# An attention and feed-forward block on one core: scores in the column tiles of the values, denominators beside the output transposes

## The reference

```
score = softmax(q k^T / sqrt(8))                # per batch and head, 1024 x 1024
out   = score v                                 # per head: 1024 x 64, seen as R = 8 rows of 8
comp  = softmax over R of ([qv, out] Ws^T + bs) # qv: 32 more query channels per head
out   = sum over R of comp * out                # 8 channels a head, 128 in all
```

## Time and profile before

| | |
|---|---|
| median of three runs | 1427.76 us |
| profiled execution, its own time | 1429.73 us |
| its span | 1428.0 us |
| PE, DVE, ACT, POOL busy | 1368.9, 1026.9, 756.1, 841.1 us |
| values, L989 | 2048 records, 558.6 us busy |
| row scores L964, column scores L981 | 1024 each, 323.6 and 313.4 us busy |
| denominators, L999 | 1024 records, 137.3 us busy |
| output transposes, L1009 | 256, 42.0 us busy |
| row maxima, L1194 | 1024, 666.5 us busy |
| exponentials, L1141 | 1024, 555.2 us busy |
| pair sums, L1294 | 256, 603.8 us busy |

### The profile page before, as it was taken

One profiled execution on the slowest core, in us unless ns is written; L12 is line 12 of the kernel. 1 busy time (PEld: TensorE's weight loads), 2 busy tenths in 40 slices (PEclk: granted clock), 3 DMA queues, 4 the chain that ended last, 5 costly groups with the idle time before them and its releaser, 6 DMA issues. The chain is left out here.

```text
span 1428.0 us, 23930 instructions
## 1 busy us (share of the span) xinstructions
PE 1368.9 (96%) x6333; PEld 436.7 (31%) x6333; DVE 1026.9 (72%) x2050; ACT 756.1 (53%) x1463; POOL 841.1 (59%) x433
## 2 busy tenths in 40 slices
PE   4699999999999999999999999999999999997898
PEld 3123222222222222222222222222222222223675
DVE  5745677877778686878777777768686868677852
ACT  4045555565555555555556555555555555563443
POOL 4235767576666766666757576665656565664321
PEclk9569999999999999999999999999999999999999
DMA  5200101010101001010101010100000000000000
GB/s 129 91 17 31 34 28 42 31 42 31 42 22 36 31 31 42 31 42 19 39 31 42 31 42 31 32 29 32 31 32 31 31 31 31 17 1 1 15 17 28
DMA packets 41937, 48.35 MB, mean 34 GB/s; under 512 B 4608, under 2 KB 23520, under 8 KB 41904
## 3 DMA queue, kind: packets, MB, share of 16 engines
q1 hardware_dynamic: 40770, 47.04, 10.0%
q0 software_dynamic: 352, 0.58, 0.3%
q10 hardware_dynamic: 782, 0.33, 0.1%
HBM read 22.51 MB, written 8.39 MB: 22 GB/s over the span
## 5 line engine op out<-in xcount | busy, mean ns | idle before, releaser
L1194 DVE TENSOR_REDUCE rowmax<-row_bank 128x1 f32<-128x512 f32 x1024 | 666.5, 684 | 319.9 <-PE row_bank L964 314.2
L1294 POOL TENSOR_TENSOR pair<-prob 128x1024 f32<-128x1024 f32 x256 | 603.8, 2359 | 452.0 <-ACT prob L1141 452.0
L1141 ACT ACTIVATE prob<-col_bank 128x512 f32<-128x512 f32 x1024 | 555.2, 594 | 463.9 <-PE col_bank L981 463.5
L989 PE MATMUL out_bank<-prob,v_op 128*64 128x512 f32 x2048 | 558.6, 624 | 0.0
L964 PE MATMUL row_bank<-k_op,q_op 72*128 72x512 bf16 x1024 | 323.6, 390 | 20.7 <-DMA v_op<-v_all 12.1
L981 PE MATMUL col_bank<-q_op,k_op 74*128 74x512 bf16 x1024 | 313.4, 387 | 0.1
L981 PEld LDWEIGHTS col_bank<-q_op,k_op 74*128 74x128 bf16 x1024 | 68.8, 98 | 332.2 <-ACT prob L1141 227.9
L989 PEld LDWEIGHTS out_bank<-prob,v_op 128*64 128x64 f32 x2048 | 101.9, 135 | 213.8 <-issue 200.5
L964 PEld LDWEIGHTS row_bank<-k_op,q_op 72*128 72x128 bf16 x1024 | 101.0, 99 | 167.6 <-DVE rowmax L1194 42.6
L999 PE MATMUL den_bank<-pair,onehot 128*32 128x512 f32 x1024 | 137.3, 608 | 0.0
L393 POOL TENSOR_TENSOR product<-mix_in,rows 128x2048 f32<-128x2048 f32 x16 | 72.5, 4529 | 2.1 <-POOLq L876 2.1
(11 more groups left out here) (183 smaller groups left out, 823.2 us busy)
## 6 DMA issues: line engine op xcount, KB each, us to landing
v_op<-v_all SPq DMA_DIRECT2D x64, 256.0 KB
k_op<-k_parts SPq DMA_DIRECT2D x64, 144.0 KB
q_op<-q_parts SPq DMA_DIRECT2D x192, 48.0 KB
q_parts<-along_parts SPq DMA_DIRECT2D x11, 192.0 KB, 2.2
k_parts<-along_parts SPq DMA_DIRECT2D x33, 64.0 KB, 2.1
out<-y_out SPq DMA_DIRECT2D x8, 256.0 KB, 2.3
q_op<-max_rows SPq DMA_DIRECT2D x64, 4.0 KB
q_parts<-first_parts SPq DMA_DIRECT2D x5, 192.0 KB, 2.1
```

The source lines that it names most:

```text
L989: last = nc.tensor.matmul(out_bank[slot % 2][ih * VW:(ih + 1) * VW, :], v_op[slot][:, t, :], halves(prob[:, t, :])[:, :, ih, :], start=(t ...
L1141: nc.scalar.activation(prob[:, t, h * HALF:(h + 1) * HALF], col_bank[h][:, :], ACT.Exp).then_inc(exp_done, 1)
L1194: nc.vector.tensor_reduce(rowmax[:, parity, t, h:h + 1], row_bank[h][:, :], AX.X, ALU.max).then_inc(max_done, 1)
L1294: pool.tensor_tensor(pair[:, k, :], prob[:, 2 * k, :], prob[:, 2 * k + 1, :], ALU.add).then_inc(pair_done, 1)
```

## The change

The row scores and the column scores are each cut into two matmuls of 64 weight columns, into partitions 0 to 63 and 64 to 127 of the same bank, with the same moving operand. The weights for the turn of the maxima are padded with zeros from 16 to 64 columns. Both denominator parts of a unit stand at t = 4 of the next one, with the output transposes behind them. ACT's copy of the turned output moves from t = 3 to t = 5, its copy of the denominators from t = 5 to t = 6, and PE's turn of them from t = 6 to t = 7. `pair` gets six tiles for four: pairs 0 and 1 alternate between two tiles each from unit to unit, pairs 2 and 3 have one each, and POOL's wait follows that. PE's wait for `denT_ready` moves from t = 7 of unit 0 to t = 4 of unit 1.

```
-        pair = sb("pair", [P, TB // 2, SEQ])
+        pair = sb("pair", [P, 6, SEQ])
+        pair_at = lambda parity, k: pair[:, 2 * parity + k if k < 2 else 2 + k, :]
-        max_parts = sb("max_parts", [P, 2, MAX_PARTS, TB], BF16)
+        max_parts = sb("max_parts", [P, 2, VW], BF16)
...
             def row_scores(v, slot, t, known_free):
-                    nc.tensor.matmul(row_bank[h][:, :], q_op[slot][0:PROD_ROWS, t * P:(t + 1) * P],
-                                     k_op[slot][0:PROD_ROWS, h * HALF:(h + 1) * HALF],
-                                     start=True, stop=True).then_inc(row_scored, 1)
+                    for c in range(2):
+                        last = nc.tensor.matmul(row_bank[h][c * VW:(c + 1) * VW, :],
+                                                q_op[slot][0:PROD_ROWS, t * P + c * VW:t * P + (c + 1) * VW],
+                                                k_op[slot][0:PROD_ROWS, h * HALF:(h + 1) * HALF],
+                                                start=True, stop=True)
+                    last.then_inc(row_scored, 1)
...
             def turn_max(w, parity):
-                nc.tensor.matmul(turn_bank[0:MAX_PARTS * TB, 0:P],
-                                 max_parts[:, parity, :, :].rearrange("p m t -> p (m t)"),
-                                 res.identb[:, :], start=True, stop=True).then_inc(max_turned, 1)
+                nc.tensor.matmul(turn_bank[0:VW, 0:P], max_parts[:, parity, :], res.identb[:, :],
+                                 start=True, stop=True).then_inc(max_turned, 1)
...
             def col_scores(u, slot, t, known_free):
-                    nc.tensor.matmul(col_bank[h][:, :], k_op[slot][0:ROWS, t * P:(t + 1) * P],
+                    for c in range(2):
+                        last = nc.tensor.matmul(col_bank[h][c * VW:(c + 1) * VW, :],
...
-                        if t == 2 and before:
+                        if t == 4 and before:
+                            if s == 1 and not first:
+                                pe.wait_ge(denT_ready, G)
+                            denominators(u - 1, sp_, 0)
+                            denominators(u - 1, sp_, 1)
                             turn_out(u - 1, sp_ % 2)
-                        if t == 4 and before:
-                            denominators(u - 1, sp_, 1)
-                        if t == 6 and s == 0 and not first:
+                        if t == 7 and s == 0 and not first:
                             pe.wait_ge(max_rows_ready, u + 2)
                             turn_den(G - 1)
...
-                        if t == 7:
-                            if s == 0 and not first:
-                                pe.wait_ge(denT_ready, G)
-                            denominators(u, s, 0)
...
             turn_out(U - 1, 1)
+            denominators(U - 1, SLOTS - 1, 0)
             denominators(U - 1, SLOTS - 1, 1)
...
-                        if t == 3 and before:
+                        if t == 5 and before:
                             if s == 1 and not first:
                                 act.wait_ge(att_done, G)
                             take_turned(u - 1, G if s > 0 else G - 1, (s - 1) % SLOTS)
-                        if t == 5 and s == 0 and not first:
+                        if t == 6 and s == 0 and not first:
                             take_den(G - 1)
...
+            dve.memset(max_parts[:, :, :], 0.0)
...
-            def pairs(u, k, known_free):
+            def pairs(u, slot, k, known_free):
                 pool.wait_ge(exp_done, 2 * TB * u + 4 * k + 4)
                 if not known_free:
-                    pool.wait_ge(den_done, 2 * u - 1 + k // 2)
-                pool.tensor_tensor(pair[:, k, :], prob[:, 2 * k, :], prob[:, 2 * k + 1, :],
+                    pool.wait_ge(den_done, 2 * u - 2 if k < 2 else 2 * u)
+                pool.tensor_tensor(pair_at(slot % 2, k), prob[:, 2 * k, :], prob[:, 2 * k + 1, :],
                                    ALU.add).then_inc(pair_done, 1)
```

More of the change, by code:

```diff
@@ L887, in attention @@
         prob = sb("prob", [P, TB, SEQ])
-        pair = sb("pair", [P, TB // 2, SEQ])
+        pair = sb("pair", [P, 6, SEQ])
+        pair_at = lambda parity, k: pair[:, 2 * parity + k if k < 2 else 2 + k, :]
         rowmax = sb("rowmax", [P, 2, TB, 2])
         negmax = sb("negmax", [P, TB])
-        max_parts = sb("max_parts", [P, 2, MAX_PARTS, TB], BF16)
+        max_parts = sb("max_parts", [P, 2, VW], BF16)
+        max_part = lambda parity, m: max_parts[:, parity, m * TB:(m + 1) * TB]
         max_rows = [sb(f"max_rows{n}", [MAX_PARTS * TB, P], BF16) for n in range(2)]
@@ L980, in col_scores @@
                         pe.wait_ge(exp_done, 2 * TB * u + 2 * t + h - 1)
-                    nc.tensor.matmul(col_bank[h][:, :], k_op[slot][0:ROWS, t * P:(t + 1) * P],
-                                     q_op[slot][0:ROWS, h * HALF:(h + 1) * HALF],
-                                     start=True, stop=True).then_inc(col_scored, 1)
+                    for c in range(2):
+                        last = nc.tensor.matmul(col_bank[h][c * VW:(c + 1) * VW, :],
+                                                k_op[slot][0:ROWS, t * P + c * VW:t * P + (c + 1) * VW],
+                                                q_op[slot][0:ROWS, h * HALF:(h + 1) * HALF],
+                                                start=True, stop=True)
+                    last.then_inc(col_scored, 1)
             def values(u, slot, t):
@@ L999, in denominators @@
                         last = nc.tensor.matmul(den_bank[q:q + 32, :], onehot[:, slot, :],
-                                                halves(pair[:, 2 * part + k, :])[:, :, ih, :],
+                                                halves(pair_at(slot % 2, 2 * part + k))[:, :, ih, :],
                                                 start=(slot == 0 and part == 0),
@@ L1089, in _ @@
                     pe.wait_ge(max_split, 1)
-                    nc.tensor.matmul(turn_bank[0:MAX_PARTS * TB, 0:P],
-                                     max_parts[:, 0, :, :].rearrange("p m t -> p (m t)"),
-                                     res.identb[:, :], start=True, stop=True).then_inc(max_turned, 1)
+                    nc.tensor.matmul(turn_bank[0:VW, 0:P], max_parts[:, 0, :], res.identb[:, :],
+                                     start=True, stop=True).then_inc(max_turned, 1)
             pe.wait_ge(onehot_set, 2)
@@ L1204, in split_max @@
                     dve.wait_ge(negmax_ready, w + 1)
-                    nc.vector.tensor_copy(max_parts[:, parity, 0, :], negmax[:, :]).then_inc(part1_ready, 1)
+                    nc.vector.tensor_copy(max_part(parity, 0), negmax[:, :]).then_inc(part1_ready, 1)
                 else:
                     dve.wait_ge(part1_ready, w + 1)
-                    nc.vector.tensor_tensor(max_parts[:, parity, 1, :], negmax[:, :], max_parts[:, parity, 0, :],
+                    nc.vector.tensor_tensor(max_part(parity, 1), negmax[:, :], max_part(parity, 0),
                                             ALU.subtract).then_inc(max_split, 1)
@@ L1300, in group @@
                     for k in range(TB // 2):
-                        pairs(u, k, first and s == 0)
+                        pairs(u, s, k, first and (s == 0 or (s == 1 and k < 2)))
                         if along and s == 0 and k == 0:
```

## The result

The changed kernel takes **1463.12 us** (median of four runs, 1461.03 to 1465.53) for 1426.69 (four runs, 1419.58 to 1430.48): 1.0262 times as long, 95% interval 1.0218 to 1.0306. 1337 was predicted, in a range of 1309 to 1385. The profiled span is 1459.2 us for 1428.0.

A forecast was written before the change was run, and what follows sets the result against it. PE was taken to bound the kernel, losing 0.25 us a plain step where column-tile width changes. Looped groups -78, first group -7.5, last -7, tail +0.4: 1429.73 - 92 = 1338 us, taken as 1337; range 1309 to 1385.

The forecast's parts named there:

- Narrow tiles, seams, loads: Plain attention step: 64-column score pairs stream in 0.217 us, loads hidden, 0.25 us of width-change seams go; 1.73 us for 1.98.
- rivals 2 to 4: Weight loads open (1412 us, 0.04); score pairs run serially (1727 us, 0.06); width costs nothing, only merging counts (1417 us, 0.04).
- Block: Denominators and output transposes together at t = 4 add 2.54 us; a plain unit takes 16.44 us for 18.47.
- Waits in the third unit: Third unit of a group: row scores wait for DVE's maxima, so only -0.4 us, -0.5 without projections; about 20.25 us.
- Moved steps: Later copies and POOL's later product in the first unit still meet every semaphore wait; no cost.
- The waits that take over: Shorter steps expose waits on DVE maxima (third unit), ACT normalizations (second, 0.35 us at t = 4), DVE work (fourth, some 0.35).
- Second: -2.0, with the projections -1.5: Second unit of a group gets 2.0 us shorter, 1.5 with projections because of transpose seams and ACT's normalizations.
- Fourth -1.65: Fourth unit of a group gets 1.65 us shorter, with some 0.35 us of DVE waits at t = 3.
- The walk of POOL's new order: POOL times from the unit's start: product to 18.1 us, pair sum 20.4, root 21.3, needed at 22.8; it holds.
- 78 shorter was predicted: Looped groups: -5.4 us each in ten with projections, -6.0 in four without, together -78.
- 7.5 predicted: First group: no mixing, so its third unit gains too; four times 1.9 us, -7.5.
- Rival 1: Plain steps become a loop of waits on row maxima: 0.1 us in some 360 steps, +36, 1374 us; chance 0.12.

The follow-up runs named there:

- run 1: Changed kernel with the split of the maxima done by four reductions instead of a DVE cast and subtraction: 1338.79 us, 0.9385 of before.
- run 9: Changed kernel with the split of the maxima by reductions and each POOL pair sum cut into two instructions of 512 columns: 1309.35 us, 0.9183 of before.
- run 5: Kernel before with only the 64-column score tiles and padded turn of the maxima; denominators, transposes and copies left in place: 1430.63 us, 0.9959 of before.
- run 6: Changed kernel with full-width scores and unpadded turn, leaving the moved block, moved copies and buffers: 1566.91 us, 1.1001 of before.
- run 7: Kernel before with scores in 64-column tiles and the split of the maxima by reductions; denominators, transposes and copies left in place: 1346.71 us, 0.9452 of before.
- run 4: Changed kernel with only the cast of the split replaced by a reduction, the subtraction kept: 1349.34 us in one run.
- run 3: Changed kernel with each POOL pair sum cut into two instructions of 512 elements, the split of the maxima unchanged: 1341.8 us in one run.
- run 2: Kernel before with the split of the maxima done by reductions: 1424.25 us, 1.0005 of before.

## Why the prediction was wrong

The forecast had chance 0.74 and its time, 1337 us, is that of run 1, not of the change; slower by more than 1% had been given 0.07. (The sum, 1337.6 less 0.14%, is 1336.) By its steps:

- **Narrow tiles, seams, loads: right.** Step 1.73 us, pairs 0.22 apart; rivals 2 to 4 are out. The pairs' weight loads stay hidden. The first rule that the prediction took from the Trainium skill ("TensorE: Matmul & The Clock Gate", Part 3, The mechanism) would have them open; here they lie over matmuls on the same rows. Whether the fast weight load was off, as its second rule says, no run here shows: it cost nothing.
- **Block: right.** The step t = 4 takes 4.31 us in a plain unit, 2.58 with 1.73 taken off; 2.54 was predicted. A plain unit is 16.43 us (unit 3 of group 0) for 16.44.
- **Waits in the third unit: right.** 20.14 us for 20.25, and 19.26 for 19.2 without projections. But the row of DVE operations was not fixed in length, as the prediction took it to be: the three large ones (L351, L361, L375) last 2.19, 1.84 and 2.16 us in before and 0.42 each at best, and run 9 takes the unit to 18.41.
- ***Moved steps*, "No cost", with *The waits that take over*: the step that failed.** Neither has a term for the split of the maxima; DVE's cast and subtraction stood at nothing, wherever POOL's sums came to lie. The walk of POOL's new order was right in its times: product to 18.41 us from the unit's start (18.1 predicted), pair sum 20.72 (20.4), root 21.40 (21.3). But it followed the semaphores only. POOL's pair sum and the next ones now lie on steps 0 to 2 of the second unit, where DVE splits the maxima, and DVE waits for POOL without a semaphore. The later copy and product are not needed for it: runs 5 and 6 show that the shorter step alone and the moved block alone each bring it about. In the fourth unit the same: cast 1.78 and subtraction 1.48 us beside POOL's two sums from 680.69 to 685.35. So the terms "Second: -2.0, with the projections -1.5" and "Fourth -1.65" were really +4.08 and +2.44 in group 7.
- **What was visible before.** The rows chosen showed no cast or subtraction at all, being short. Before has both where POOL pauses in the second unit, and in the fourth one cast of 0.56 us that ends with a pair sum:

```profile
674.51 0.56 DVE L1205 CAST max_parts<-negmax 128x8 bf16<-128x8 f32 x1
```

```profile
672.68 2.36 POOL L1294 TENSOR_TENSOR pair<-prob 128x1024 f32<-128x1024 f32 x1
```

  672.68 + 2.36 = 675.04, 674.51 + 0.56 = 675.07. With the 2.16 us of the earlier trace rows, for an operation that takes 0.42 elsewhere, that was enough to ask.
- **Where the 31 us lie.** Groups 1 to 14 are 1118.43 - 1070.28 = 48.2 us longer (78 shorter was predicted), and 2.2 lie ahead of group 0 and from group 15 on. Group 0 is 87.25 - 68.12 = 19.1 us shorter (7.5 predicted), 13.6 of them in its first unit, 29.89 us at a clock of 0.50 in before and 16.32 at 0.83 in after. That part is luck of the profiled executions and hides some of the loss.
- **Rival 1** came nearest, with PE waiting for row maxima, and was still wrong: not 0.1 us in each of 360 steps, but 2 to 3 us at one place in half of the units, and it called for the second maximum of a plain step, which is in time.
- **The clock** had no term. Against run 1, PE waits 95.0 - 22.7 = 72 us more for row maxima. The mean clock of 0.946 over 1459.2 us, if all that is missing was spent at half clock, means (1 - 0.946) x 2 x 1459.2 = 158 us there, and 0.981 over 1337.1 means 51; the 107 us between them cost half, 53. By this estimate it is 126 together, for 124.3 measured. Why the clock falls after such a wait in one unit and not in another stays open.
- **Two errors that cancelled in run 1.** Groups 1 to 14 gave 1070.28 - 999.58 = 70.7 us for 78 predicted, since the row scores of step t = 2 wait 0.15 us in each unit (1.88 us for 1.73). That wait comes with the fourth reduction of run 1; in the plain units of after the step takes 1.73. Group 0 gave 18.1 for 7.5: in before its first unit ran at a clock of 0.50, 29.89 us; in run 1 it took 16.98. That the sum met run 1 within 2 us is luck in part.

## What to carry to other kernels

When an edit moves an engine's long instructions in time, it isn't enough to follow the semaphores: look at what DVE does beside POOL. An instruction whose longest duration is ten times its shortest (view by tile or line: minimum, median, maximum), ending where a POOL instruction ends, is waiting; do it as a reduction or put it elsewhere, or cut POOL's instructions. And give a wait of PE a range: in run 5 the same 2.17 us cost 19.65 - 17.51 = 2.1 us where the clock held and 24.37 - 17.51 = 6.9 where it fell (17.51 is the unit in run 7).

## What the runs showed of the hardware

- In before and after, the split's casts and two-operand instructions that begin while a pair sum of POOL runs end with it (0.16 us alone, up to 2.27 beside a sum of 2.36 us; 2.34 in runs 4 and 5); reductions beside the same sum take 0.15 to 0.17 us. A root of POOL of 128 x 2 elements didn't hold them up (0.16 to 0.19 us in run 4).
- It goes the other way as well. Where DVE's long instruction came first, POOL's took longer, here 2.66 us for 2.35 in before; in run 3 the half sums that begin while L351, L361 or L375 runs take 1.45 us for 1.27:

```profile
1273.31 0.69 DVE L507 TENSOR_TENSOR above<-above,below 128x512 f32<-128x512 f32 x1
```

```profile
1273.56 2.66 POOL L1294 TENSOR_TENSOR pair<-prob 128x1024 f32<-128x1024 f32 x1 [2.39 <-ACT prob L1141]
```

- The clock was 0.50 for 5.5 us after a PE wait of 2.37 us in one unit of after. In run 5 it fell in one unit with 2.17 us of idle time (0.79 in the mean) and stayed at 1.00 in the next with as much. In the very first unit, before's profile has 0.50 throughout, while run 2's, with the same instructions on PE, has 0.70 and takes 22.04 us for 29.89; these 7.85 us account for the difference of the two spans (1428.0 and 1420.2). The runs of before lie between 1419 and 1431 us, the shortest with a mean clock of 0.983, the longest of 0.975 or 0.976, worth some 10 us by the same estimate. What decides the clock of the first unit was not tried.
